# Two attentions on one core: row maxima in tiles of 1024 keys, exponentials in tiles of 512, the hand-over of the maxima on ScalarE by query halves

## The reference

```python
x = x + _L0_conv_ref(_gn(x), ...)          # attention 1, on group-normalised x
t = t + _L1_attn_ref(_ln_t(t), ...)        # attention 2, on layer-normalised tokens
t = t + _L1_ffn_ref(_ln_t(t), ...)         # 16 experts, top 1
# inside attention 1, for b in 8, n in 12 heads, L = 1024, hd = 16:
attn = jnp.einsum('bhqd,bhkd->bhqk', q * scale, k)
rel_h = jnp.einsum('bnhwd,hkd->bnhwk', rq, Rh)
rel_w = jnp.einsum('bnhwd,wkd->bnhwk', rq, Rw)
attn = (attn.reshape(B, nh, H, W, H, W) + rel_h[..., :, None] + rel_w[..., None, :]).reshape(B, nh, L, L)
attn = jax.nn.softmax(attn, axis=-1)
out = jnp.einsum('bhqk,bhkd->bhqd', attn, v)
# attention 2: the same without the relative terms, scores divided by sqrt(192)
```

## Time and profile before

| what | us |
|---|---|
| median of 3 runs (lowest, highest) | 3238.24 (3232.71, 3240.13) |
| span of the profiled execution, first to last instruction | 3278.2 |
| PE busy | 2922.2 (89%) |
| DVE busy | 2439.8 (74%) |
| ACT busy | 1849.7 (56%) |
| POOL busy | 1061.6 (32%) |
| attention 1, first scores to last copy of the output | 365.00 to 1459.64 |
| attention 2, the same | 1796.40 to 2843.47 |

### The profile page before, as it was taken

One profiled execution on the slowest core, in us unless ns is written; L12 is line 12 of the kernel. 1 busy time (PEld: TensorE's weight loads), 2 busy tenths in 40 slices (PEclk: granted clock), 3 DMA queues, 4 the chain that ended last, 5 costly groups with the idle time before them and its releaser, 6 DMA issues. The chain is left out here.

```text
span 3278.2 us, 63755 instructions
## 1 busy us (share of the span) xinstructions
PE 2922.2 (89%) x17818; PEld 1147.0 (35%) x17818; DVE 2439.8 (74%) x4430; ACT 1849.7 (56%) x2379; POOL 1061.6 (32%) x1714
## 2 busy tenths in 40 slices
PE   5886999999999999977897999999999999871887
PEld 4664122222222222215652222222222222361666
DVE  4544899999999999933547999999999999451221
ACT  2433376667776677663440677777777777610332
POOL 0012233333333333213232333232333332155665
PEclk9776799999999999998995999999999999965777
DMA  6776554555445554433654622222222222350211
GB/s 126 219 237 184 104 103 98 100 110 107 102 101 100 111 103 100 90 61 121 206 160 98 124 72 70 72 75 75 73 76 75 70 71 63 97 89 12 58 54 35
DMA packets 222364, 327.92 MB, mean 100 GB/s; under 512 B 63820, under 2 KB 150550, under 8 KB 217650
## 3 DMA queue, kind: packets, MB, share of 16 engines
q0 software_dynamic: 79488, 202.00, 27.3%
q1 hardware_dynamic: 142772, 124.60, 14.5%
HBM read 217.71 MB, written 109.19 MB: 100 GB/s over the span
## 5 line engine op out<-in xcount | busy, mean ns | idle before, releaser
L458 ACT ACTIVATE a_probs<-a_psS 128x1024 f32<-128x1024 f32 x1536 | 1488.5, 1021 | 738.5 <-PE a_psS L371 734.0
L503 DVE TENSOR_REDUCE h_halfmax<-a_psR 128x1 f32<-128x512 f32 x1536 | 979.7, 686 | 73.5 <-PE a_psR L353 64.3
L503 DVE TENSOR_REDUCE a_halfmax<-a_psR 128x1 f32<-128x512 f32 x1536 | 984.2, 686 | 63.6 <-PE a_psR L353 54.5
L371 PE MATMUL a_psS<-a_qrows,a_krows 121*128 121x512 f16 (+1 forms) x3072 | 804.2, 383 | 44.8 <-DMA a_qrows<-relh 40.2
L382 PE MATMUL a_psO<-a_probs,a_v 128*32 128x512 f32 x6144 | 824.0, 609 | 1.2 <-ACT a_probs L458 1.2
L353 PE MATMUL a_psR<-h_kmax,h_qmax 64*128 64x512 f16 x1536 | 357.9, 405 | 40.8 <-POOL h_ident L39 40.1
L371 PEld LDWEIGHTS a_psS<-a_qrows,a_krows 121*128 121x128 f16 (+1 forms) x3072 | 241.8, 98 | 417.7 <-issue 161.5
L353 PE MATMUL a_psR<-a_kmax,a_qmax 64*128 64x512 f16 x1536 | 325.6, 393 | 1.8 <-DVE a_halfmax L503 1.4
L353 PEld LDWEIGHTS a_psR<-h_kmax,h_qmax 64*128 64x128 f16 x1536 | 81.9, 93 | 539.1 <-DVE h_halfmax L503 471.6
L353 PEld LDWEIGHTS a_psR<-a_kmax,a_qmax 64*128 64x128 f16 x1536 | 78.9, 93 | 490.4 <-DVE a_halfmax L503 460.1
L185 POOL DMA_DIRECT2D a_qrows<-qk x240 | 124.1, 517 | 264.5 <-PE a_psO L382 262.0
(11 more groups left out here) (185 smaller groups left out, 2755.2 us busy)
## 6 DMA issues: line engine op xcount, KB each, us to landing
a_qrows<-qk POOLq DMA_DIRECT2D x240, 128.0 KB, 4.2
qk<-p_half SPq DMA_DIRECT2D x96, 256.0 KB, 3.3
a_qrows<-rel POOLq DMA_DIRECT2D x96, 256.0 KB, 4.2
a_v<-v POOLq DMA_DIRECT2D x96, 256.0 KB, 3.1
a_krows<-qk POOLq DMA_DIRECT2D x168, 128.0 KB, 4.5
v<-p_v SPq DMA_DIRECT2D x36, 512.0 KB, 5.7
relh<-p_rel SPq DMA_DIRECT2D x48, 256.0 KB
attn<-a_out SPq DMA_DIRECT2D x96, 128.0 KB, 2.3
```

What stands on the lines that cost most here:

```text
L371: mm = nc.tensor.matmul(psS[:, (2 * n + j) % 4, :], K[buf][:, h, keys], A[buf][kt % NA][:, h, queries], start=True, stop=True)
L458: nc.scalar.activation(PT[:, blk % 2, 2 * pair:2 * pair + 2, :], psS[:, b0:b0 + 2, :], ACT.Exp, scale=scale).then_inc(exped, 1)
L503: nc.vector.tensor_reduce(mx[:, unit, half:half + 1], psR[:, slot, :], AX.X, ALU.max)\
```

## The change

- **Max jobs.** A job is now one unit over all 1024 keys: two matmuls, one on partitions 0 to 63 with keys 0 to 511, one on 64 to 127 with keys 512 to 1023, into one of two double banks of `psR`, and one reduction of 1024 values. A block has two jobs (L335) instead of four: one before the values, one late. DVE's joining step falls away.
- **Scores and exponentials** go by single banks, three of them: four score matmuls (L349), each with its own wait, and four exponentials of 512 (L466). The order on PE is: scores 0 and 1, a max job, the values of the block before (L369), scores 2, a max job, scores 3.
- **The copy of `psO`** (L445) stands between the exponentials of heads 2 and 3 of blocks 0 and 8; it stood behind all exponentials of the block.
- **The hand-over** is done by halves of the queries, in block 5 for the second half of the same step and in block 13 for the first half of the next: four transposes of 128x4 into a bank of `psS` (L359), a scaled copy on ACT (L451) between exponentials 2 and 3, and a DMA one block later.
- **The prologue** holds 22 jobs (16 units of the first half, 6 of the second) instead of 76; only the last 11 blocks have no max jobs.
- **Loads** are spread otherwise: q in blocks 0 to 2, the relative terms in 3 to 5, k in 6 to 8, v in 9 and 10, operands of maxima in 6 to 13. The height rows are fetched by two DMAs a block, one for each pair of heads.

Cut to its core, the diff is:

```diff
-    HALVES = 2 * UNITS
-    PER_BLK = HALVES // BLK
-    MAXBLK = BLK - 3
-    EARLY = PER_BLK * (BLK - MAXBLK)
+    HALF = UNITS // QH
+    PER_BLK = UNITS // BLK
+    NEXT = 5
+    AHEAD = NEXT + HALF // PER_BLK
+    EARLY = PER_BLK * (BLK - AHEAD)
+    RING = 2
+    BANKS = 3
...
-        psS = ctx.enter_context(nc.psum_tensor(f"{name}_psS", [P, 4, 512], F32))
-        psR = ctx.enter_context(nc.psum_tensor(f"{name}_psR", [P, 3, 512], F32))
+        psR = ctx.enter_context(nc.psum_tensor(f"{name}_psR", [P, RING, 1024], F32))
+        psS = ctx.enter_context(nc.psum_tensor(f"{name}_psS", [P, BANKS, 512], F32))
...
-                offset, j = (1, EARLY + PER_BLK * blk) if blk < MAXBLK else (2, PER_BLK * (blk - MAXBLK))
-                if not (last and u + offset >= 2):
-                    after[blk] += [("max", j + i, offset) for i in range(PER_BLK)]
-            if not (last and u == 1):
-                after[MAXBLK].insert(2, ("rows",))
-            after[KT + 2].append(("back", 0, 0))
-            if not (first and u == 0):
-                after[2].append(("back", -1, 1))
-            if last and u == 1:
-                after[BLK].append(("back", 0, 1))
-            return after
-        FIRST = [("max", j, 0) for j in range(HALVES)] + [("rows",)] + [("max", j, 1) for j in range(EARLY)]
-        PROLOGUE = len(FIRST)
+                if blk < NEXT:
+                    offset, j = 0, HALF + EARLY + PER_BLK * blk
+                elif blk < AHEAD:
+                    offset, j = 1, PER_BLK * (blk - NEXT)
+                else:
+                    offset, j = 1, HALF + PER_BLK * (blk - AHEAD)
+                if not (end and offset):
+                    at_once[blk].append(("max", j, offset))
+                    later[blk].append(("max", j + 1, offset))
+            if end:
+                later[BLK].append(("back", 0, 1))
+            return at_once, later
+        PROLOGUE = HALF + EARLY
...
+            def load(s, buf, blk):
+                if rel:
+                    if blk < 3:
+                        load_query(s, buf, 0, blk)
+                        load_query(s, buf, 1, blk)
+                    elif blk < 5:
+                        load_width(s, buf, 0, blk - 3)
+                        load_width(s, buf, 1, blk - 3)
+                    elif blk == 5:
+                        load_height(s, buf, 0)
+                        load_height(s, buf, 1)
+                    elif blk < 9:
+                        load_key(s, buf, blk - 6)
+                elif blk < 8:
+                    (load_query(s, buf, 0, blk // 2) if blk % 2 == 0 else load_key(s, buf, blk // 2))
+                if blk in (9, 10):
+                    load_values(s, buf, blk - 9)
...
+                if rel and 6 <= blk < 14:
+                    head.load_rel(pool, s, AM[buf], KM[buf], loadedm[buf], (blk - 6) % 2, (blk - 6) // 2)
+                if not rel and 6 <= blk < 14:
+                    head.load_terms(pool, s, AM[buf], KM[buf], loadedm[buf], blk % 2, (blk - 6) // 2)
...
+            def row_of_maxima(buf, qh, unit):
+                sp.wait_ge(exped, unit + 1)
                 for c in range(NA):
-                    sp.dma_start(A[buf][c][R:R + 1, :, :].rearrange("o h (t q) -> o (h t) q", q=P), MT[:, :])\
-                      .then_inc(mrow, 16)
-            def rel_rows(s, buf, blk):
+                    sp.dma_start(A[buf][c][R:R + 1, :, 512 * qh:512 * qh + 512], MT[:, qh, :]).then_inc(mrow, 16)
...
-                sp.wait_ge(scores, s * SCORES + 2 * (blk - 2) + 2)
-                cols = slice(512 * qh, 512 * qh + 512)
-                sp.dma_start(A[buf][c][RH:RH + 8, :, cols],
-                             RLH[s, kt].rearrange("i (k h) t -> (i k) h t", h=GH)[:, :, cols]).then_inc(relrow[c], 16)
+                sp.wait_ge(scores, s * SCORES + place(blk - 2, 2 * pair + 1) + 2)
+                cols, of = slice(512 * qh, 512 * qh + 512), slice(2 * pair, 2 * pair + 2)
...
+                    if blk == NEXT + 1:
+                        row_of_maxima(u, 1, s * SCORES + place(NEXT, GH - 1))
+                    if blk == AHEAD + 1 and more:
+                        row_of_maxima(1 - u, 0, s * SCORES + place(AHEAD, GH - 1))
                     if rel and blk % KT < KT - 2:
-                        rel_rows(s, u, blk + 2)
+                        rel_rows(s, u, blk + 2, 0)
+                        rel_rows(s, u, blk + 2, 1)
...
-                    r, half, p, qt, _ = max_of(j[1])
+                    h, qt = unit_of(j[1])
                     b = (buf + j[2]) % 2
-                    at = slice(64 * r, 64 * r + MR)
-                    mm = nc.tensor.matmul(psR[:, slot, :], AM[b][half][at, p, P * qt:P * qt + P],
-                                          KM[b][at, p, 512 * half:512 * half + 512], start=True, stop=True)
-                elif j[0] == "rows":
-                    pe.wait_ge(maxed, rows + 1)
-                    mm = nc.tensor.transpose(psR[0:UNITS, slot, 0:P], MC[:, :], ident[:, :])
+                    for r in range(2):
+                        at = slice(MR * r, MR * r + MR)
+                        mm = nc.tensor.matmul(psR[:, slot, 512 * r:512 * r + 512], AM[b][at, h, P * qt:P * qt + P],
+                                              KM[b][at, h, :], start=True, stop=True)
...
-            def scores_pair(buf, kt, qh, pair, n, pairs):
-                pe.wait_ge(exped, pairs + n + 1)
-                for j in range(2):
-                    keys, queries = slice(P * kt, P * kt + P), slice(512 * qh, 512 * qh + 512)
-                    h = 2 * pair + j
-                    mm = nc.tensor.matmul(psS[:, (2 * n + j) % 4, :], K[buf][:, h, keys], A[buf][kt % NA][:, h, queries],
-                                          start=True, stop=True)
+            def score(s, buf, kt, qh, h, m, first):
+                if not (first and m < BANKS - 1):
+                    pe.wait_ge(exped, s * SCORES + (m + 2 - BANKS))
+                keys, queries = slice(P * kt, P * kt + P), slice(512 * qh, 512 * qh + 512)
+                nc.tensor.matmul(psS[:, bank(m), :], K[buf][:, h, keys], A[buf][kt % NA][:, h, queries],
+                                 start=True, stop=True).then_inc(scores, 1)
+            def row(half, m, reduced, free):
+                pe.wait_ge(ring_free, reduced + RING + 1)
+                if free is not None:
+                    pe.wait_ge(exped, free)
+                for t in range(KT // QH):
+                    at = HALF * half + GH * t
+                    mm = nc.tensor.transpose(psS[0:GH, bank(m), P * t:P * t + P], MC[:, at:at + GH], ident[:, :])
...
-                    scores_pair(u, kt, qh, 0, 2 * blk, 2 * blks)
-                    scores_pair(u, kt, qh, 1, 2 * blk + 1, 2 * blks)
-                    some(js[:2])
-                    last_pv()
-                    some(js[2:])
-                if last and u == 1:
-                    pv(u, BLK - 1, blks, halves)
-                    for jn, j in jobs[u][BLK]:
-                        job(jn, j, base, slot(jn), free(jn), u, halves, s + 1)
+                        for n, j in part:
+                            job(n, j, base, (n + shift) % RING, u, s * QH)
+                    def two_scores(pair):
+                        if rel and kt >= 2:
+                            pe.wait_ge(relrow[blk % 2][pair], s * (16 * NREL) + 16 * (3 * qh + kt // 2))
+                        score(s, u, kt, qh, 2 * pair, place(blk, 2 * pair, end), start)
+                    two_scores(0)
+                    score(s, u, kt, qh, 1, place(blk, 1, end), start)
+                    some(at_once)
+                    if blk >= 1:
+                        pv(s, u, blk - 1, end)
+                    elif not start:
+                        pv(s - 1, 1 - u, BLK - 1, False)
+                    two_scores(1)
+                    some(later)
+                    if blk == NEXT:
+                        m = place(blk, GH - 1, end) - 1
+                        row(1, m, base + number_of(jobs, u, ("max", UNITS - 1, 0)), s * SCORES + (m + 2 - BANKS))
+                    if blk == AHEAD and not end:
+                        m = place(blk, GH - 1, end) - 1
+                        row(0, m, base + number_of(jobs, u, ("max", HALF - 1, 1)), s * SCORES + (m + 2 - BANKS))
+                    score(s, u, kt, qh, GH - 1, place(blk, GH - 1, end), start)
...
-                for n in range(2 * BLK):
-                    blk, pair = n // 2, n % 2
-                    act.wait_ge(scores, s * SCORES + n + 1)
-                    act.wait_ge(pvdone, s * PVS + blk + 1)
-                    b0 = 2 * n % 4
-                    nc.scalar.activation(PT[:, blk % 2, 2 * pair:2 * pair + 2, :], psS[:, b0:b0 + 2, :], ACT.Exp,
-                                         scale=scale).then_inc(exped, 1)
-                    if n == 1 and not (first and u == 0):
-                        copy_out(s - 1, 1, before(u - 1, 1))
-                    if n == 2 * KT + 1:
```

(32 more changed lines are left out.)

326 lines of the change are left out of this document (149 added, 177 removed).

## The result

The changed kernel takes **3321.16 us** (median of 4 runs, 3318.45 to 3324.36), the kernel before 3235.47 (4 runs): ratio **1.027**, 95% interval 1.0254 to 1.0288.

What follows compares the result with a forecast made beforehand. PE was taken to bound the kernel. Parts 1 to 3 gave 104 us an attention, +208, prologue -37, height rows -20: +151 us, 3389 us; own range 3325 to 3445, wider range 3290 to 3455.

Steps and rivals of the forecast that it cites:

- What bounds the kernel: Whole loop: PE sets the 2.61 us block and waits for nobody; DVE could do a block in 2.40 us.
- Part 1, the five groups: Steady block on PE: a fifth group adds a change of kind, 0.11 us, making the block 2.72 us.
- Part 2, the chain through ACT: Scores 2 to values through exponential 3: 2.71 to 2.79 us, 2.75 taken; with the last blocks +64 us an attention.
- rival B: Steady block: the fifth change is free and the chain hides, block stays 2.61 us, total 3238; chance 0.10.
- Part 3: Work now inside the chain, copy and hand-over: +16.5 and +23.5 us an attention, back job 0.
- The copy: ACT's output copy, now ahead of exponential 3: 0.35 us each, 47 times, +16.5 us an attention.
- The hand-over: Hand-over blocks: exponential 3 starts 0.79 us later, 47 times, 37.1 us against 13.6 before, +23.5 net an attention.
- The transposes: Hand-over on PE: four transposes take 0.50 us, with one more change of kind 0.61.
- The back job: Back-job blocks: cost 0.62 us before and delay scores 3 by the same now, so 0 net.
- Part 4, the prologue: Before first scores: 22 reductions of 1024 give -19.3 us in attention 2, -18 in attention 1, together -37.
- Part 5, the height rows: Attention 1's 40.2 us of PE waits for height rows: -20 us taken, between -40 and +20.
- Rival C: Height rows: paired fetches and bunched loads make PE wait, attention 1 40 to 80 us more, total 3450 to 3500; chance 0.08.

Runs made afterwards that it cites:

- e2: Kernel before, with each reduction over 256 of its 512 keys, leaving out the other half's maxima: 3171.20 us, ratio 0.981.
- e1: Kernel before, with the second pair of scores behind the first two max jobs, five groups a block: 3478.43 us, ratio 1.077.
- e5: Kernel before, with the second pair of scores behind the first two max jobs and reductions over 256 of 512 keys: 3278.53 us, ratio 1.015.
- e4: Changed kernel, with both max jobs in one group and scores 2 behind them, four groups a block: 3268.00 us, ratio 1.011.
- e10: e4, with the row of maxima between max jobs and scores 2, and attention 1's row issued ahead of second-buffer constants and eight POOL loads: 3222.09 us, ratio 0.997.
- e8: Kernel before, with POOL's loads moved to blocks near the changed kernel's, k with q in blocks 0 to 2: 3325.82 us, ratio 1.030.
- e9: Kernel before, with height rows fetched by two heads and PE waiting for each ahead of its pair of scores: 3219.78 us, ratio 0.996.
- e12: e10, with the whole loads of height rows in block 6 and no longer in block 5: 3203.78 us, ratio 0.993.
- e11: Kernel before, with the whole loads of height rows in block 6 and no longer in blocks 8 and 9: 3311.16 us, ratio 1.027.

## Why the prediction was right, and where its numbers were off

**What bounds the kernel: right** for the steady block, by e2. The prediction's "it waits for nobody" holds there alone; e2 shows 20 us an attention in which PE waited for DVE and the ring elsewhere.

**Part 1, the five groups: right, to the hundredth.** 2.72 from the starts of the tail rows; 2.72 in the trace; e1, e5 and e4 put it on and took it off. A single score matmul was followed 0.32 later, as foretold. The fifth groups come to 80 us (2 x 365 x 0.11); the other terms nearly cancel.

**Part 2, the chain through ACT: the term was mis-sized.** The chain had bounds of 2.71 and 2.79, and I took 2.75. The two bounds came from two times between a score matmul and its exponential, 0.43 in the tail and 0.505 in the old loop. The lower one holds: scores 2 start at 2152.71 and exponential 2 at 2153.14, 0.43 later. So exponential 3 can start 0.43 behind scores 3, at 1.08, it lasts 0.60 (the 0.59 that I took was right), and the values start at 1.72, the very time at which PE reaches them. The chain is as long as PE's own sum and costs nothing; in this, rival B was right. The difference is 365 x 0.03, 11 us an attention. (Exponentials of 512 that wait for nothing follow each other 0.49 apart, three in 1.59.) The tail came out as described. Timeline of the changed kernel, last blocks:

```profile
2916.85 1.06 PE L369 MATMUL a_psO<-a_probs,a_v 128*32 128x512 f32 x8
...
2919.41 1.07 PE L369 MATMUL a_psO<-a_probs,a_v 128*32 128x512 f32 x8
```

2.56 a block, where the prediction had 2.55, and 1.96 before.

**Part 3.** The copy: 0.41 instead of 0.35, through the wait named. The hand-over: 0.91 instead of 0.79, a near hit with the wrong wait, and so in part luck. I had exponential 3 delayed, and it was: it started at 2171.72, 1.84 behind scores 2, where 1.86 to 1.96 were foretold. But another wait ended later, that for the bank of the row, which the prediction never asked about, though the change makes `psS` a ring of three and puts the row into it. Exponential 3 would have let the values start near 2172.35; the bank let them start at 2172.51. In e4 the chain has slack, and the hand-over costs as much, by the bank alone. The transposes were over-priced, at 0.61: they take 0.43, since the change of kind added for them isn't paid. The back job: taken as 0 net, in truth 0.44 instead of 0.62; 47 x 0.18 = -8.5 us. With DVE relieved (e2) the back block of the kernel before is 0.13 shorter, so most of the 0.18 was a wait for the ring that is gone. And before, every second step lost 0.47 us at its block 0, where the loop turns over; after, that loss isn't seen: -5 us.

Parts 1 to 3 were to give 104 us an attention. They gave 81.8 in attention 2; the differences named above make about 17 of the 22 that are missing, and the rest isn't traced. Attention 1 took 47.5 us more than attention 2 before (1094.6, 1047.1) and 1.1 less after. The height rows thus cost 47.5 and not the 40.2 of PE's idle times, which leave out part of each wait and the halved clock behind four of them (last section). So parts 1 to 3 gave 33.1 + 47.5 = 80.6 there, in all **162 and not 208**.

**Part 4, the prologue.** Attention 2: -20.2 (foretold -19.3). Attention 1: -9.3 and not -18. I had seen that SP was busy with constants, and had let the row land at once behind them. It was issued at 347.79 and used 11.6 us later, where 4.4 were allowed. (The prologue itself began 3.7 us later than before, at 322.27, so the issue came only 1.6 us later in it than foretold.) The failed step is the landing: a small DMA was priced as in the loop. In e10, with SP's constants and eight of POOL's loads behind it, it was issued at 342.97 and used 4.2 us later. Which of the two, constants or loads, held it up is not shown, as no run moved one alone.

**Part 5, the height rows.** -47.5 and not -20, beyond the end of the range (-40); even PE's idle times alone are at that end. The reason given (loads of q and k moved away from block 10) may be near the truth, but it isn't shown: in e8, where q and k moved together, the waits went with them. Of the two things that the changed kernel does otherwise, fetches by pairs give 13 to 16 us alone (e9); parting k from q was never tried alone. Rival C didn't come: attention 1 of the changed kernel shows no wait for height rows.

The sum: +151 foretold, +86 measured; -46 from parts 1 to 3, -27 from the height rows, +8 from the prologue. No term had the wrong sign, and the price that decided, 0.11 us for a change of kind, was read from rows. Still the measured time lies just outside the forecast's own range: the two large misses went the same way.

## What to carry to other kernels

Count on the bound engine not only the work but the changes of kind between groups, and read their price from two rows with and without one: here 0.11 us each made a change slower that took 7% of the work from DVE, and regrouping gave it back (e4). When a result moves into another ring of banks, ask who waits for that bank, and for the last reduction in front of it; both are as real as the chain one looks at. And the time at which a load is issued says little: ask what is already on the DMA engines, since a small DMA that is needed soon can land late behind it (11.6 us against 4.2, 5.8 for a fetch in the loop).

The best kernel of this study is e12, 3203.78 us: 0.7% faster than the kernel before and 117 us under the changed one (108 if each is set against the kernel before on its own chip), with the changed kernel's tiles and hand-over in four groups a block.

## What the runs showed of the hardware

- Two DMAs of 4 KB were used 11.6 us after their issue (347.79 to 359.38) while the loads of POOL and SP were on the engines, against 4.2 us (342.97 to 347.17) with eight of POOL's loads and eleven of SP's issued later.
- A wait of PE can cost more than its length. In e11 PE waited 23 times in attention 1, 2.47 to 3.67 us each, and each wait went with a stretch at half the clock (1.2 GHz). Timeline and window of e11:

```profile
595.46 1.88 PE L375 MATMUL a_psS<-a_qrows,a_krows 121*128 121x512 f16 x4 [3.60 <-DMA a_qrows<-relh]
...
595.40:600.00 4.60, 4.54 (x16) 0.84 (x16) 1.29 (x2) 1.94 (x2) 0.00 (x0) 0.50 0.17 45
```

  These scores took 1.88 us instead of 1.04. The waits in attention 1 grew by 39 us against the kernel before, but the attention by 77 (1171.2 against 1094.6). Shorter waits did it less often: in the kernel before, 19 of 23 waits (1.51 to 1.91 us, the one at 582.65 among them) left the clock at 1.00, and four (1.72, 1.92, 2.31 and 2.40 us) were followed by a stretch at 0.50. Timeline of the kernel before, one of the four:

```profile
396.52 1.70 PE L371 MATMUL a_psS<-a_qrows,a_krows 121*128 121x512 f16 x4 [2.31 <-DMA a_qrows<-relh]
```

- The idle time in front of a score row understates a wait: 0.32 shown at 2171.87, 0.49 by the starts.
- Reductions of 1024 values follow each other 1.14 us apart (25.00 us for 22 in the prologue of attention 2), those of 512 0.60: the wide form saves 5% of DVE's time, no more.
